# A decoder layer with a mixture of experts: early tiles from four groups, up products of 224, 384 or 512 columns, and exponentials by tile

## The reference

```python
x = x + linear_attention(layernorm(x))          # 8 heads, elu(q)+1, elu(k)+1
x = x + cross_attention(layernorm(x), ctx)      # scores (x - mean) / (std + eps), softmax over 77, @ v, @ Wout
# mixture of experts on layernorm(x), E = 8, K = 2
logits = x @ Wg.T
top_v, top_i = top_k(logits, 2)
gates = softmax(top_v, axis=-1)
cap = int(4096 * 2 * 1.25 / 8)                  # 1280
pos = position of each assignment within its expert, in token order
keep = pos < cap                                # what is beyond is dropped
h = einsum('ecd,edf->ecf', exp_batches, W1)     # 512 -> 2 x 1024
inp, gate = split(h, 2)
exp_out = einsum('eci,eid->ecd', gelu(inp) * gate, W2)   # 1024 -> 512
out = segment_sum(gates * exp_out[...], token)
x = x + out
```

## Time and profile before

| | |
|---|---|
| median of 3 runs | 1474.22 us |
| lowest, highest | 1474.14, 1477.27 us |
| the profiled execution's own time | 1474.55 us |
| its span in the trace | 1472.8 us |
| PE busy | 1430.7 us (97%) |
| DVE, ACT, POOL busy | 640.8, 591.7, 374.8 us |
| mean granted clock of PE | 0.993 |

### The profile page before, as it was taken

How to read it: one execution, slowest core, us unless ns; L and a number is a source line. 1 busy time by engine, 2 the same in 40 slices (tenths; PEclk the granted TensorE clock), 3 DMA queues, 4 the chain that set the end, 5 groups by cost and what they waited for, 6 DMA issues and landing times.

```text
span 1472.8 us, 22222 instructions
## 1 busy us (share of the span) xinstructions
PE 1430.7 (97%) x7508; PEld 1210.8 (82%) x7509; DVE 640.8 (44%) x1379; ACT 591.7 (40%) x1018; POOL 374.8 (25%) x365
## 2 busy tenths in 40 slices
PE   7999999989989999999999999999999999999997
PEld 5768887778876888889889888899889888898886
DVE  7535666657777563123524421166223420253111
ACT  5534554258776552223424421255323321252212
POOL 3302232137666412203202211121301111021111
PEclk9999999999998999999999999999999999999999
DMA  6331223218658764204505421156504412052112
GB/s 206 60 64 30 86 87 58 86 33 209 172 133 221 176 186 108 42 2 85 151 34 123 107 64 34 21 157 189 132 7 118 103 57 43 7 152 54 21 36 28
DMA packets 82854, 135.64 MB, mean 92 GB/s; under 512 B 33234, under 2 KB 33362, under 8 KB 81780
## 3 DMA queue, kind: packets, MB, share of 16 engines
q1 hardware_dynamic: 65428, 97.68, 23.2%
q0 software_dynamic: 17376, 37.30, 13.8%
HBM read 94.41 MB, written 40.55 MB: 92 GB/s over the span
## 4 chain that ended last, share of the span: by engine, by line
PE 90%; DVE 3%; ACT 2%; issue 2%; DMA 1%; POOL 1%; SPq 0%; POOLq 0%; DVEq 0%; ACTq 0%
PE pg L1050 16%; PE pg L1052 16%; PE pg L1051 16%; PE pj L1050 10%; PE pj L1051 10%; PE pj L1052 10%; PE pj L1289 2%; PE pg L1317 2%; PE pt L1458 2%; PE pg L1255 2%; PE pt L1276 1%; PE pt L1071 1%; DMA out_rows<-ost,etab 1%; DVE kf L1582 1%; PE pt L1201 1%
## 5 line engine op out<-in xcount | busy, mean ns | idle before, releaser
L1050 PE MATMUL pg<-xe_hi,w_hi 128*128 128x512 f32 (+2 forms) x1152 | 401.7, 349 | 3.0 <-DVE xe_lo L1534 1.9
L1051 PE MATMUL pg<-xe_lo,w_hi 128*128 128x512 f32 (+2 forms) x1152 | 401.1, 348 | 0.0
L1052 PE MATMUL pg<-xe_hi,w_lo 128*128 128x512 f32 (+2 forms) x1152 | 401.0, 348 | 0.0
L1994 DVE TENSOR_TENSOR hp<-gl,pg 128x512 f32<-128x512 f32 x136 | 93.5, 688 | 569.9 <-ACT gl L1021 569.9
L728 POOL DMA_INDIRECT out_rows<-ost,etab x62 | 99.6, 1606 | 721.7 <-ACT ost L1005 359.0
L1021 ACT ACTIVATE gl<-pg 128x512 f32<-128x512 f32 x136 | 81.3, 598 | 410.9 <-PE pg L1052 410.9
L1050 PEld LDWEIGHTS pg<-xe_hi,w_hi 128*128 128x128 f32 x1152 | 218.5, 190 | 29.0 <-issue 2.8
L1051 PEld LDWEIGHTS pg<-xe_lo,w_hi 128*128 128x128 f32 x1152 | 218.5, 190 | 25.0
L1052 PEld LDWEIGHTS pg<-xe_hi,w_lo 128*128 128x128 f32 x1152 | 218.5, 190 | 25.0
L1050 PE MATMUL pj<-w_hi,hg_hi 128*128 128x512 f32 x448 | 177.0, 395 | 0.0
L1052 PE MATMUL pj<-w_hi,hg_lo 128*128 128x512 f32 x448 | 174.5, 389 | 0.0
(11 more groups left out here) (250 smaller groups left out, 1992.8 us busy)
## 6 DMA issues: line engine op xcount, KB each, us to landing
stage<-w SPq DMA_DIRECT2D x96, 512.0 KB, 4.1
xr<-x SPq DMA_DIRECT2D x8, 1024.0 KB, 10.6
out_rows<-xr SPq DMA_DIRECT2D x8, 1024.0 KB, 7.3
x_rows<-xn SPq DMA_DIRECT2D x8, 1024.0 KB, 7.1
x_in<-x SPq DMA_DIRECT2D x7, 1024.0 KB, 6.0
x_rows<-zrow POOLq DMA_DIRECT2D x1, 2304.0 KB, 15.7
late_xT<-xT_hi SPq DMA_DIRECT2D x2, 1024.0 KB, 3.9
late_xT<-xT_lo SPq DMA_DIRECT2D x2, 1024.0 KB, 6.0
```

The source lines that it names most:

```text
L1050: nc.tensor.matmul(o, lh, rh, start=start, stop=False)
L1051: nc.tensor.matmul(o, lh, rl, start=False, stop=False)
L1052: return nc.tensor.matmul(o, ll, rh, start=False, stop=stop)
L1994: v.tensor_tensor(hp[j % 2][:], gl[j % 2][:], pg[:, 2 + j % 2, :], ALU.mult).then_inc(s_hp, 1)
```

## The change

Four things are changed together.

1. **Widths.** The list `UP_WIDTHS` is 224, 384 and 512. The smallest that holds `left` is taken. The early steps keep their 256 columns.
2. **Early tiles from four groups.** `SOON` is 4 instead of 6: the table's first 256 slots are read back and their rows gathered in group 4. `turn_soon` stands in group 5, ahead of `positions(5)`; the row halves have buffers of their own (`soon_xe_hi`, `soon_xe_lo`). Zeros are stored for the rows of four groups and 128 more, 17 tiles instead of 9. Early step 0 stands ahead of `turn_exp(6)`, step 1 ahead of `turn_exp(7)` with three dummies instead of six; they write other PSUM banks (`pj[1]`, `pt[1]`), and `positions` changes its bank with the group. The other six steps stay behind group 7. Weight pieces 0 and 1 are requested in group 5, 2 and 3 in group 6, 4 and 5 behind group 6's store; 6 on as before, behind group 7's. ACT and DVE split them at new places.
3. **Exponentials by tile.** Each exponential has its own semaphore step, and each transpose of `turn_exp` waits for its own tile.
4. **Small steps.** `sigma` on POOL is one operation instead of two, with the factor moved to DVE's next one; the gate is made with Tanh of minus half the difference and two scalings, instead of Exp, an addition, a reciprocal and a product.

The core of the diff:

```diff
+UP_WIDTHS = [2 * P - 32, 3 * P, 4 * P]
...
-SOON, SOON_TILES = GROUPS - 2, 2
+SOON, SOON_TILES = GROUPS - 4, 2
+SOON_TURNED = SOON + 1
+EARLY_UPS = 2
...
+        def soon_x(j):
+            return (pj[1], pt[1])[j][:, 0:SOON_SLOTS] if j < EARLY_UPS else pg[:, j % 2, 0:SOON_SLOTS]
...
             for g in range(GROUPS):
+                if g == SOON_TURNED:
+
+                    sp.wait_ge(s_o, (GROUPS - 1) * TI)
+                    first_pieces(range(EARLY_UPS))
                 if g == GROUPS - 2:
 
                     sp.wait_ge(s_o, GROUPS * TI)
-                    first_pieces(range(STG))
+                    first_pieces(range(EARLY_UPS, STG))
...
-                if g == SOON:
+                if g == GROUPS - 2:
                     first_pieces(range(STG, STG + 2))
                 if g == GROUPS - 1:
                     first_pieces(range(STG + 2, STG + 6))
...
-                step(p.tensor_scalar(sig[:, 0], mv2[:, :, 1], CK / (CK - 1.0), None, ALU.mult))
-                p.tensor_tensor(sig[:, 1], sig[:, 0], half_pos[:], ALU.pow).then_inc(s_sig, 1)
+                p.tensor_tensor(sig[:, 1], mv2[:, :, 1], half_pos[:], ALU.pow).then_inc(s_sig, 1)
...
-                a.activation(ge[:], gd[:], ACT.Exp).then_inc(s_ge, 1)
+                a.activation(ge[:], gd[:], ACT.Tanh, scale=-0.5).then_inc(s_ge, 1)
...
                 for i in range(TI):
-                    ins = a.activation(sc[:, i, :], sc[:, i, :], ACT.Exp, bias=nbias[:, i:i + 1],
-                                       scale=sig[:, 3, i:i + 1])
-                ins.then_inc(s_e, 1)
+                    a.activation(sc[:, i, :], sc[:, i, :], ACT.Exp, bias=nbias[:, i:i + 1],
+                                 scale=sig[:, 3, i:i + 1]).then_inc(s_e, 1)
...
+                if g == SOON_TURNED:
+                    act.wait_ge(s_proj, JA + LATE)
+                    split(0, 0)
+                    rows_hi(0, range(SOON_TILES), soon_xe_hi)
+                if g == GROUPS - 2:
+                    split(0, EARLY_UPS)
                 if g == GROUPS - 1:
-                    rows_hi(0, range(SOON_TILES))
-                    for s in range(2, STG):
+                    for s in range(STG, STG + 2):
                         split(0, s)
+                    for j in range(EARLY_UPS):
+                        soon_gelu(j)
                 squares_3(g)
+                if g == SOON_TURNED:
+                    split(0, 1)
...
             def turn_exp(g):
-                pe.wait_ge(s_e, g + 1)
                 to = bank(0)
                 for i in range(TI):
+                    pe.wait_ge(s_e, g * TI + i + 1)
                     ins = nc.tensor.transpose(to[0:CK, i * P:(i + 1) * P], sc[:, i, :], ident[:])
...
+                if g == GROUPS - 2:
+                    pe.wait_ge(s_posev, g)
+                    pe.wait_ge(s_qfree, LATE)
+                    pe.wait_ge(s_xelo, SOON_TILES)
+                    soon_up(0)
                 if not more_groups:
 
                     pe.wait_ge(s_posev, g)
-                    for _ in range(6):
-                        mm(pj[1][:], ident[:], wqk[:].rearrange("p k c -> p (k c)")[:, 0:512], start=True, stop=True)
+                    soon_up(1)
+                    pe.wait_ge(s_x2t, g * TI)
+                    for _ in range(3):
+                        mm(pg[:, 3, :], ident[:], wqk[:].rearrange("p k c -> p (k c)")[:, 0:512], start=True, stop=True)
...
-                if not more_groups:
+                if g == SOON_TURNED:
                     turn_soon()
-                    positions(g)
+                positions(g)
...
+                    if g == SOON_TURNED:
+                        rows_lo_of(0, range(SOON_TILES), soon_xe_lo, soon_xe_hi)
+                        split(0, 0)
                     score_stats(g + 1)
...
-                    with pe.If(left < 2 * P + 1):
-                        up(2)
-                    with pe.Else():
-                        with pe.If(left > 3 * P):
-                            up(4)
+                    def up_narrowest(widths):
+
+                        if len(widths) == 1:
+                            up(widths[0])
+                            return
+                        half = len(widths) // 2
+                        with pe.If(left < widths[half - 1] + 1):
+                            up_narrowest(widths[:half])
                         with pe.Else():
-                            up(3)
+                            up_narrowest(widths[half:])
+
+                    up_narrowest(UP_WIDTHS)
```

More of the change, by code:

```diff
@@ L953, in _ @@
                     late_q(late(g, 1))
[L956 to L960, removed]
-                    a.activation(gl[j % 2][:, 0:SOON_SLOTS], pg[:, j % 2, 0:SOON_SLOTS], ACT.Gelu).then_inc(s_gl, 1)
-                if j >= 1:
-                    act.wait_ge(s_hp, j)
-                    a.activation(soon_hi[:, j - 1, :], hp[(j - 1) % 2][:, 0:SOON_SLOTS], ACT.Copy).then_inc(s_hghi, 1)
-                if j == 0:
-                    split(0, STG)
+            for j in range(1, FJ + 1):
+                if EARLY_UPS < j < FJ:
+                    soon_gelu(j)
+                act.wait_ge(s_hp, j)
+                a.activation(soon_hi[:, j - 1, :], hp[(j - 1) % 2][:, 0:SOON_SLOTS], ACT.Copy).then_inc(s_hghi, 1)
                 if j == 1:
-                    split(0, STG + 1)
                     split(0, STG + 2)
@@ L981, in _ @@
                 if i == 0:
-                    rows_hi(SOON_TILES, range(CHUNKS[0]))
+                    rows_hi(SOON_TILES, range(CHUNKS[0]), xe_hi)
             act.wait_ge(s_meta, 1)
@@ L1258, in attend @@
                     ins.then_inc(s_o, 1)
-            nt, last = [0], [0, 0]
+            nt, last, soon_turned = [0], [0, 0], [0, 0]
             def bank(k):
@@ L1341, in turn_soon, with soon_up @@
                     ins.then_inc(s_xet, 1)
+                    soon_turned[i] = i + 1
+            def soon_up(j):
+                pe.wait_ge(s_w_lo, j + 1)
+                for to, half in ((soon_x(j), 0), (soon_gate(j), 1)):
+                    m = slice(half * P, (half + 1) * P)
+                    for k in range(KC):
+                        ins = three(to, w1_hi[:, j, k, m], w1_lo[:, j, k, m],
+                                    soon_xe_hi[:, k, :], soon_xe_lo[:, k, :], k == 0, k == KC - 1)
+                ins.then_inc(s_h, 1)
             attend(0, range(2))
@@ L1389, in turn_first_rows @@
                     ins.then_inc(s_xet, 1)
[L1392 to L1396 removed]
+            for j in range(EARLY_UPS, FJ):
+                if j < EARLY_UPS + 2:
+                    pe.wait_ge(s_x2t, GROUPS * TI - 1 + j - EARLY_UPS)
                 else:
                     pe.wait_ge(s_hp, j - 1)
[L1399 to L1404 removed]
+                soon_up(j)
             at_e, at_c, at_left, at_first, at_done, at_next = (
@@ L1436, in _, with up @@
                     following = pe.snap(first + 2 + (c < 2) * 2, min_val=2, max_val=EX * ET + 14)
[L1438 to L1440 removed]
+                    def up(w):
                         pe.wait_ge(s_xelo, following)
@@ L1907, in _ @@
                 else:
-                    for s in range(2):
+                    for s in range(EARLY_UPS, STG):
                         split(0, s)
+                if g == GROUPS - 2:
+                    split(0, 1)
                 if more_groups:
@@ L1923, in _ @@
                     cross_out(g)
-                    rows_lo_of(0, range(SOON_TILES))
                     positions_out(g)
                     slots(g)
-                    split(0, 2)
+                    for j in range(EARLY_UPS):
+                        soon_product(j)
+                    split(0, STG)
                     gate_diff(g)
-                    split(0, 3)
                     pack_tokens(g)
+                    soon_product_lo(0)
+                    split(0, STG + 1)
             def counts():
```

93 lines of the change are left out of this document (50 added, 43 removed).

## The result

The changed kernel takes 1492.66 us (median of 4, 1489.38 to 1493.69), the kernel before 1474.18 in the same rounds: a ratio of 1.0117, with a 95% interval of 1.0096 to 1.0139, or 18.5 us slower. Slower was forecast, by 8.8 us and at most 1488.5; the time lies above that range. The profiled execution took 1493.5 us with a span of 1491.8, 19.0 more than the span before. The ratios in this document leave out one execution, of `branch_never_taken`, that took 1530.63 us and lay more than 1.5% above the fastest of its kernel.

The account below looks back on a forecast made before the run. It took PE's matmuls to bound the expert loop, and waits and a cold clock to matter around groups 6 and 7. 1474.55 + 15.6 - 7.0, less 0.3, gave 1483.0 us; range 1476.5 to 1488.5.

Parts of the forecast that it names:

- The widths, +15.6: Expert loop: two third chunks go from 256 to 384 columns, +20.5 us; three chunks from 256 to 224, -4.9.
- Groups 0 to 2, -1.5: Softmax of groups 0 to 2: transposes by tile overlap ACT's exponentials, saving 0.5 us a wait.
- Group 5, +1.6: Early tiles' eight transposes move into group 5: 1.03 us, plus 0.6 waiting for their buffer.
- group 6 up to the scores of group 7: Gains and losses around group 6 cancel; group 7's scores come when they came before, bounds -2 to +2 us.
- Group 7, -4.2: Transposes gone, value products warm, no wait for rows: the next early step starts near 468.2 instead of 472.37.
- a filled wait keeps the clock: Groups 6 and 7: PE, no longer idle, may keep its clock; value products take 3.76 us instead of 5.54.
- The six early steps, 22.6 us: Behind group 7: 17.3 us at pace plus about 5.3 of waits, against 26.30 for eight before; another -3.7.
- the front: Everything ahead of the expert loop: -7.0 us in all, with ends of -13.2 and -3.5.
- The gathers, 6 to 7 us earlier: Gathers of expert 0's rows come 6 to 7 us earlier, not 8, so early output tiles give 0.9 back.
- the third: Rival, 12%: the front gives next to nothing, -1 us instead of -7, total 1489 us.
- the lowest, -3.5: The front's small end: -3.5 us if the clock falls as before and the weights come late.
- Added at no cost: Larger zero store (4352 KB instead of 2304), Tanh gate and earlier early weight pieces cost nothing.

Follow-up runs that it names:

- branch_never_taken: Kernel before plus a fourth branch of up products, 32 columns wide, that no chunk takes: 1.0207 of the kernel before, times from 1496 to 1531 us.
- widths_alone: Kernel before with only its list of widths changed to 224, 384, 512: 1490.81 us, 1.0115 of the kernel before.
- front_alone: Changed kernel with 256 in place of 224 in its list of widths: 1474.33 us, 0.9993 of the kernel before.
- steps_behind_group_7: front_alone with pieces 6 and 7 requested earlier, ACT's last normalisation later, one more dummy, and early steps 0 and 1 behind group 7: 1468.33 us, 0.9961.

## Why the prediction was wrong

- **The widths, +15.6: right.** +16.6 measured in `widths_alone` alone. The chunks that moved are those named, 33.31 us is what a 384-column one takes, and the narrow pace is 111.7 ns where 111.5 was taken from the spacing of weight loads. The 106.7 ns estimated from the Trainium skill ("TensorE: Matmul & The Clock Gate", section "LDWEIGHTS (loading the stationary operand)") are 5 ns under the measurement, which decides.
- **Groups 0 to 2, -1.5: the sum about right, the cause wrong.** They gave 0.44 us each (21.12 less 20.68). The prediction put this on the transposes, which give 0.06, and laid POOL's step in the same waits at no gain of its own, where it was nearly all.
- **Group 5, +1.6, and group 6 up to the scores of group 7: right.** 1.06 and 0.71 us in group 5, and the scores of group 7 at 451.56 against 451.78.
- **Group 7, -4.2: its warm clock failed.** Expected were warm value products, 3.76 us instead of 5.54. In the changed kernel's profiled execution they took 7.17, which is the whole difference between 468.2 and 471.62. In that of `front_alone` they were cold too (5.45), and that its third step came at 468.14 is luck: its scores of group 7 began at 450.09, 1.7 us sooner than forecast. The step said that a filled wait keeps the clock; but the step and the dummies filled the time ahead of the transposes, and the gap of 0.68 us after them is left by the change; with one dummy there the products took 3.68 us.
- **The six early steps, 22.6 us: failed, and this is the step that undid the front.** They took 28.25, and about 29.3 in `front_alone`, where the step before them and the gathers behind them were in time. The prediction saw that pieces 6 to 9 are requested behind the last group's store and took 7.7 us for a piece to land and 5.3 us for all waits, with a warm clock. Piece 6 took 9.9 us (11.63 in `front_alone`), one wait alone is 6.60 (7.12), and behind it PE ran at 0.50 from 488.30 to about 494. It had put the wait on ACT's order and the piece together, but counted no clock lost behind it: 28.25 less 17.3 less 6.6 leaves 4.3 us for cold matmuls at both ends.
- **The gathers, 6 to 7 us earlier: came, but bound nothing.** They start 6.2 us earlier in `front_alone` and, behind the longer value products, 2.7 in the changed kernel (498.39 instead of 501.12). In the kernel before and in both of these, expert 0 starts 13.9 us behind the first product of the early output tiles, so the 0.9 that the prediction had the gathers give back was not called on.
- **The sum.** -4.2 - 3.7 + 0.9 = -7.0 became +1.16 (-1.09 in `front_alone`), and the cold products behind expert 0's chunk added 1.64 in the profiled execution. The rival that came was the third, at -1 us; the range had cut off its far half, and no case had the front losing time; the lowest, -3.5, already had the clock fall as before and the weights come late.
- **Added at no cost** held: the larger zero store took 19.9 us and nobody waited for it.

What stays open: why a piece takes 9.9 to 14.4 us to land in this place instead of 7.7; what besides the two short gaps decides whether group 7's value products run cold; why the clock fell behind expert 0's narrow chunk in the changed kernel's profiled execution and not in that of `widths_alone`, with the same chunk. Nor was it tried which of the front's other parts bring the 5.8 us that `steps_behind_group_7` has over the kernel before: it has the early requests, the dummies, the shorter softmax chain and the rows from four groups together.

## What to carry to other kernels

Work that is moved into a wait only pays if what comes after it is ready as much sooner: follow the next inputs (here a weight piece whose request stood behind a store) before the gain is counted, and count a new pause twice where the matmuls behind it may run cold. A list of sizes has to hold the sizes that caps make common: 256 left of a capacity of 1280 was the one to keep, and a size more in a loop that is written out can cost more than it saves: here 26 us net, where the narrow chunks were to save 4.8.

## What the runs showed of the hardware

- A fourth written-out branch in the expert loop, never taken, made the kernel 2% slower: the instruction queue moved 1.20 MB instead of 0.49, and PE waited up to 5.7 us for its own instructions ahead of the chunks and ran at a mean clock of 0.98 instead of 1.00.
- 0.3 and 0.7 us of idle time around short matmuls at 461 and 463 us were followed by the clock's lower level from 464 to 474. In four kernels with a dummy product of 1.02 us in the second gap it stayed at 1.00, and in four of ten without one.
- Matmuls of 224 columns ran 111.7 ns apart, 8.3 below those of 256. The line through 256 and 384 columns would give 106.6; 111 ns is the spacing of the 128-column weight loads ahead of 9-column matmuls, so the loads are taken to set the pace. No run had fewer columns.
- Weight pieces of 512 KB, requested among the last group's stores, took 9.9 us to land in the changed kernel and 10.2 to 14.4 in seven edits of it (the piece through which the chain that ended last goes), against 4.1 in the median over the whole kernel before.
